# Weight halves split inside attention steps, and earlier places for the last two row groups, in a fused embed, text, attention and expert kernel

## What is computed

```
h = concat(patch_embedding(x), text_layers(x_txt))            # 32 x 114 x 256
h = h + attention(layernorm(h))                               # causal, 128-wide q and k
n = layernorm(h)
logits = n @ w_router.T;  top_vals, top_idx = top_k(logits, 2)
rw = softmax(top_vals)
y_e = (silu(n @ w_gate[e].T) * (n @ w_up[e].T)) @ w_down[e].T    # e = 0..7, FFN 512
out = sum over the two chosen e of rw * y_e
h = h + (layernorm(out) * ln_gamma + ln_beta)
```

## Time and profile before

| | us |
|---|---|
| median of 3 runs | 1122.44 (1122.32 to 1122.86) |
| the profiled execution: its time | 1125.7 |
| the profiled execution: span from first to last instruction | 1123.9 |
| busy in that span: PE, DVE, ACT, POOL | 975.9, 758.9, 601.9, 577.5 |
| mean granted TensorE clock, as a share of full speed | 0.939 |

### The profile page before, as it was taken

The page is one execution under the profiler, slowest core; times in us unless marked ns, Lnnn a source line. Parts: engine busy times, 40 slices in busy tenths (PEclk is TensorE's granted clock), DMA queues, the critical chain, the costliest instruction groups (busy, mean ns, idle before and its releaser), DMA issues.

```text
span 1123.9 us, 20592 instructions
## 1 busy us (share of the span) xinstructions
PE 975.9 (87%) x5838; PEld 846.4 (75%) x5839; DVE 758.9 (68%) x1966; ACT 601.9 (54%) x1343; POOL 577.5 (51%) x630
## 2 busy tenths in 40 slices
PE   5878999999999999999898962499999999999910
PEld 4668999999999999998666652377777777777710
DVE  1666999999999998998678767244444444444447
ACT  1466776877788777666697753123223223223223
POOL 4523765567667766777627767232222222222236
PEclk8998999999999999999999975699999999999965
DMA  9451001000100000012168236133233333333263
GB/s 278 130 151 57 1 1 66 1 2 1 67 1 2 1 25 2 10 58 57 36 212 260 61 76 224 52 47 50 47 47 49 49 47 47 47 50 48 43 162 118
DMA packets 54733, 75.49 MB, mean 67 GB/s; under 512 B 9348, under 2 KB 46978, under 8 KB 52612
## 3 DMA queue, kind: packets, MB, share of 16 engines
q1 hardware_dynamic: 32680, 49.24, 14.5%
q0 software_dynamic: 16640, 18.53, 10.1%
q10 hardware_dynamic: 5340, 6.83, 2.2%
HBM read 45.38 MB, written 29.14 MB: 66 GB/s over the span
## 4 chain that ended last, share of the span: by engine, by line
PE 68%; DVE 10%; POOL 7%; DMA 5%; issue 4%; ACT 3%; SPq 2%; POOLq 0%; ACTq 0%; DVEq 0%
PE bank L1264 16%; PE bank L1580 10%; PE bank L1329 7%; PE bank L1557 6%; PE bank L1566 5%; PE bank L1565 4%; PE bank L1324 3%; POOL xrows L1174 3%; PE bank L1560 3%; PE bank L1572 2%; DMA xtok<-in_tok_emb,tokens_s 2%; PE bank L1312 2%; SPq L541 1%; POOL xtok L1052 1%; DVE arena_b L1736 1%
## 5 line engine op out<-in xcount | busy, mean ns | idle before, releaser
L1203 POOL DMA_INDIRECT yrows<-arena_b,dest_i x64 | 99.2, 1550 | 268.2 <-ACT arena_b L1009 260.3
L1736 DVE SCALAR_TENSOR_TENSOR arena_b<-bank,sml,arena_b 128x304 f32<-128x304 f32 (+2 forms) x384 | 195.3, 522 | 20.7 <-ACT arena_b L778 17.9
L1264 PE MATMUL bank<-xt_hi,w_hi 128*128 128x308 f32 x512 | 159.9, 312 | 4.6 <-DVE arena_b L1736 3.2
L1264 PE MATMUL bank<-xt_hi,w_lo 128*128 128x308 f32 x512 | 157.3, 307 | 0.0
L1264 PE MATMUL bank<-xt_lo,w_hi 128*128 128x308 f32 x512 | 156.9, 306 | 0.0
L2057 DVE TENSOR_TENSOR arena_b<-bank,arena_b 128x512 f32<-128x512 f32 x64 | 44.3, 691 | 140.5 <-PE bank L1566 76.7
L1090 POOL TENSOR_TENSOR u_halves<-arena_b,u_halves 128x308 fp32r<-128x308 f32 x128 | 109.8, 865 | 29.8 <-ACT arena_b L790 29.7
L1084 POOL TENSOR_TENSOR y_lo<-arena_b,y_hi 128x308 fp32r<-128x308 f32 x128 | 107.9, 857 | 27.2 <-ACT y_hi L802 27.0
L1264 PEld LDWEIGHTS bank<-xt_hi,w_hi 128*128 128x128 f32 x512 | 98.0, 191 | 5.4 <-DVE arena_b L1736 3.5
L1580 PE MATMUL bank<-arena_b 128*128 x384 | 98.7, 393 | 1.2 <-DVE arena_b L2073 0.9
L1264 PEld LDWEIGHTS bank<-xt_hi,w_lo 128*128 128x128 f32 x512 | 98.0, 191 | 0.0
(11 more groups left out here) (212 smaller groups left out, 2650.3 us busy)
## 6 DMA issues: line engine op xcount, KB each, us to landing
arena_b<-xrows SPq DMA_DIRECT2D x64, 129.5 KB, 2.1
wg_raw<-in_w_gate SPq DMA_DIRECT2D x4, 1024.0 KB, 7.1
yrows<-arena_b SPq DMA_DIRECT2D x1, 3648.0 KB, 18.7
h_all<-seq SPq DMA_DIRECT2D x8, 448.0 KB
w_raw<-in_w_in SPq DMA_DIRECT2D x3, 1024.0 KB, 4.8
arena_b<-in_w_down SPq DMA_DIRECT2D x3, 1024.0 KB, 8.6
wu_raw<-in_w_up SPq DMA_DIRECT2D x2, 1024.0 KB, 7.3
wu_s<-in_w_up SPq DMA_DIRECT2D x2, 1024.0 KB, 9.4
```

The costliest lines, as they stand in the source:

```text
L1203: pool.indirect_dma_start(yrows, bass.IndirectOffsetOnAxis(ap=dest_i[:, m:m + 1], axis=0), f_y[m % 2], None, compute_op=ALU.add).then_inc( ...
L1264: mm = pe.matmul(out_, in_half(w, layer, d, slice(c * P, (c + 1) * P)), x[:, d, cols], start=(k == 0), stop=(k == len(pairs) - 1))
L1736: dve.scalar_tensor_tensor(acc[:, :, back_:TXT], x[:, :, 0:TXT - back_], conv_w(s // GROUPS, c, tap), acc[:, :, back_:TXT], ALU.mult, ALU. ...
```

## The change

It does three things.

1. Pieces 0 to 3 of the weights are split inside the attention steps: ACT does 0 and 1 in step 2 and 2 and 3 in step 3, behind the first norm of the next group and ahead of the tanh. DVE does piece 0 in step 2 ahead of the choice, piece 1 at the end of step 2, pieces 2 and 3 in steps 3 and 4 ahead of the choice.
2. Pieces 4 and 5 stay behind the table on DVE, but wait now until POOL has issued its last row send (the semaphore `pad_zero` gets a new name and a second increment for that). PE waits for four pieces before its first block and for the other two before the up product of block 0.
3. From step 8 on, the ranks and the places of a group stand in the same step as its choice, behind it: group 6 in step 8 and group 7 in step 9, where they stood one step later. Step 8 keeps the places of group 5 at its start.

```diff
--- before.py
+++ after.py
@@ -336,7 +336,9 @@
         assert at[0] <= 3 * FC * GT
 
         EMBEDDED = 5
-        SPLIT_FIRST = 3
+        SPLIT_FIRST = 4
+        SPLIT_STEP = 2
+        LOWER_AT = {2: 0, 3: 2, 4: 3}
         BIAS_OPS = 3 * 3 + 11
         LAST_LAG = 3
         SENT_FIRST = 5
@@ -472,7 +474,7 @@
         a_om, a_h2 = sem("a_om"), sem("a_h2")
         m_stats, m_rstd, m_norm, m_tr, m_trc = sem("m_stats"), sem("m_rstd"), sem("m_norm"), sem("m_tr"), sem("m_trc")
         m_lm, m_gap, m_wt, m_both, m_rk = sem("m_lm"), sem("m_gap"), sem("m_wt"), sem("m_both"), sem("m_rk")
-        m_slot, pad_zero = sem("m_slot"), sem("pad_zero")
+        m_slot, zeroed_then_sent = sem("m_slot"), sem("zeroed_then_sent")
         a_bias, m_bias, ld_qkv = sem("a_bias"), sem("m_bias"), sem("ld_qkv")
         x_sent = [sem(f"x_sent{k}") for k in range(ROW_SETS)]
 
@@ -966,6 +968,9 @@
                     key(g)
                 if has(g + 1):
                     norm_rows(g + 1)
+                if g in (SPLIT_STEP, SPLIT_STEP + 1):
+                    for k in range(2):
+                        upper_weights((g - SPLIT_STEP) * 2 + k)
                 if has(g - 2):
                     weight(g - 2)
                 if has(g):
@@ -976,9 +981,6 @@
                     rows_turned(g + 1, 1)
                 if has(g):
                     gate_values(g, 1)
-                if g - 1 == GROUPS - 1:
-                    for k in range(SPLIT_FIRST):
-                        upper_weights(k)
                 if has(g - 1):
                     routed_norm(g - 1)
 
@@ -1185,7 +1187,7 @@
                 if has(g + 2):
                     norm_ahead(g + 2)
                 if g == 0:
-                    pool.memset(padbuf[:, :], 0.0).then_inc(pad_zero, 1)
+                    pool.memset(padbuf[:, :], 0.0).then_inc(zeroed_then_sent, 1)
                 if has(g - 1):
                     routed_scale(g - 1)
                 if has(g - 3):
@@ -1194,6 +1196,8 @@
             for g in range(GROUPS + LAST_LAG):
                 attn_step(g)
 
+
+            settled(pool, zeroed_then_sent)
 
             def send(j, m, landed):
                 pool.wait_ge(f_yc, j + 1)
@@ -1507,7 +1511,7 @@
                 if has(g - 2):
                     turn_routed(g - 2, 0)
                     turn_routed(g - 2, 1)
-                if has(g - 3):
+                if has(g - 3) and g <= GROUPS:
                     ranks(g - 3)
                 if has(g):
                     values(g, 0)
@@ -1525,6 +1529,8 @@
                     values(g, 1)
                 if has(g + 1):
                     bias_scores(g + 1)
+                if has(g - 2) and g >= GROUPS:
+                    ranks(g - 2)
 
             bias_scores(0)
             for g in range(GROUPS + LAST_LAG):
@@ -1537,7 +1543,7 @@
 
             pe.wait_ge(tbl_ready, 2)
             pe.wait_ge(ld_ffn, 16 * (len(FFN_PIECES) + FC))
-            pe.wait_ge(w_lower, len(FFN_HALVES))
+            pe.wait_ge(w_lower, SPLIT_FIRST)
 
             def turn_block(j, k, turn_):
                 pe.wait_ge(x_in[k], turn_ * 16 + 16)
@@ -1561,6 +1567,8 @@
                 mm.then_inc(f_gm, 1)
                 wait(pe, f_hh, j)
                 pe.wait_ge(f_raw, j + 1)
+                if isinstance(j, int) and j == 0:
+                    pe.wait_ge(w_lower, len(FFN_HALVES))
                 for x, w in ((x_lo, wu_hi), (x_hi, wu_hi), (x_hi, wu_lo)):
                     pe.matmul(bank[1][:, :], x[:, k, 0, :], w[:, cols], start=(x is x_lo), stop=False)
                 pe.matmul(bank[1][:, :], x_raw[k], wu_s[:, cols], start=False, stop=True).then_inc(f_um, 1)
@@ -1915,7 +1923,7 @@
 
             def routed_stats(g):
                 if g == 0:
-                    dve.wait_ge(pad_zero, 1)
+                    dve.wait_ge(zeroed_then_sent, 1)
                     dve.tensor_copy(padbuf[:, D:D + 1], cst[:, C_PADDEST:C_PADDEST + 1]).then_inc(pad_ready, 1)
                     for half in range(2):
                         dve.wait_ge(seq_stored[2 + half], 16 * len(rows_out[half]) * GROUPS // 2)
@@ -1982,15 +1990,14 @@
 
             text_iterations(text_step)
             def attn_step(g):
-                if has(g - 3):
+                if has(g - 3) and g <= GROUPS:
                     place_rows(g - 3)
                 if has(g + 1) and g:
                     norm_bias(g + 1)
                 if has(g + 2):
                     norm_ahead_stats(g + 2)
-                if g - 2 == GROUPS - 1:
-                    for k in range(SPLIT_FIRST):
-                        lower_weights(k)
+                if g in LOWER_AT:
+                    lower_weights(LOWER_AT[g])
                 if has(g - 2):
                     choose(g - 2)
                 if has(g):
@@ -2003,9 +2010,13 @@
                     count(g - 2)
                 if has(g - 1):
                     routed_bias(g - 1)
+                if has(g - 2) and g >= GROUPS:
+                    place_rows(g - 2)
                 if has(g):
                     invert(g)
                     weigh(g)
+                if g == SPLIT_STEP:
+                    lower_weights(1)
 
             for g in range(GROUPS + LAST_LAG):
                 attn_step(g)
@@ -2046,6 +2057,7 @@
             dve.tensor_copy(expert_i[:, :], expert_f).then_inc(tbl_ready, 1)
             c.done()
             dve.wait_ge(tbl_ready, 2)
+            dve.wait_ge(zeroed_then_sent, 2)
             for k in range(SPLIT_FIRST, len(FFN_HALVES)):
                 lower_weights(k)
```

## The result

The changed kernel takes **1137.07 us** (median of four, 1131.94 to 1140.74), the kernel before beside it 1122.43: a ratio of **1.0116** (95% interval 1.0095 to 1.0138), slower by 14.6 us. Two further sets of the same kernel, taken later on two chips, gave 1.0135 and 1.0131. The forecast was 1133.5, with a range of 1130.0 to 1138.5: the time is inside, and 3.6 us above the point.

A forecast was written before the change was run, and what follows sets the result against it. The bound was taken as a ring of ACT, PE and DVE, then POOL's row sends from 682 us. A shift of +18.2 less 7.1 at the end gave +11.1 us: median 1133.5, range 1130 to 1138.5.

The forecast's parts named there:

- The stall: Step 2: ACT stands 8.0 us for the first two weight loads; with the copies the ring shifts 12.0 us.
- The other pieces: Piece 1's lower half and pieces 2 and 3, steps 2 to 4: shift grows from 12.0 to 18.2 us.
- The shift at the end of step 4: Total delay of the attention steps from the stall and pieces 0 to 3: 18.2 us.
- The end: POOL's last sends, up to the first expert transpose: 2.1 us of idle and slowed sends go, 7.1 us gained.
- all six are now alone: End: the six sends formerly beside pieces 0 to 5 meet no lower half, saving 2.7 and 2.3 us.
- The slow sends: POOL sends beside DVE's lower halves: pieces 2 and 3 lengthen one or two sends, 0.8 to 1.6 us a piece.
- The sum: Whole kernel: +18.2 us of shift less 7.1 us at the end, +11.1 us, median 1133.5.
- The clock: PE's granted clock after its idle time in step 2: counted as nothing, ACT and DVE hiding a slow PE.
- The rival: Clock stays low in two or three steps where PE is waited for: +3 to +5 us, 1136.5 to 1138.5; chance 0.11.
- The other rivals: No stall (1125.5, chance 0.05); no gain at the end (1140.6, 0.05); not slower, by packed sends (1122.8, 0.07).
- the ring: Attention steps, first half: ACT, PE and DVE release each other, 14.5 us a step, no engine alone the bound.
- packing its queue: Not-slower rival: POOL's sends packed without waits for slots give back 10.7 us, about 1122.8; chance 0.07.

The follow-up runs named there:

- the profile with the memset: Changed kernel, with the bare increment that frees DVE's pieces 4 and 5 replaced by a small POOL memset behind its last send: 1135.96 us, ratio 1.0110.
- the repeated run: The changed kernel again without an edit, on two chips: 1140.87 us, ratio 1.0135, and 1138.83 us, ratio 1.0131.

## Why the prediction was right, and where it was not

**The stall: right.** 8.0 us were worked out from when SP issues its third load; 8.00 were measured, released by the load named. The exact hit is luck: the wait was 7.83 and 8.24 us in the changed kernel's other profiles, and 6.09 and 6.78 in two others with the same pieces in step 2. Step 2 is 12.6 us longer (the tanh comes 12.2 later, 12.0 were forecast; the rest is part of piece 1). With the pieces one step later the stage is 6.8 us shorter than in the profile after, though its clock fell for longer in step 4.

**The other pieces: right, a little too large.** Steps 3 and 4 together are 5.0 us longer; 6 was forecast. The shift at the end of step 4 is 17.6 us (18.2). The first send comes at 597.72, which with the 5.1 us of the text stage added is 602.8 (603).

**The end: one step failed.** "Pieces 4 and 5 wait for the end of POOL's last send" and "all six are now alone" are not what the semaphore does. The increment was done at least eleven microseconds ahead of the last send's end, and the pieces slowed two sends by 2.1 us. The Trainium skill (PSUM — Partial Sum Buffer, section "Engine vs sequencer instructions") gives the reason: a bare semaphore operation runs on the sequencer and doesn't wait for the instructions ahead of it to complete. The trace agrees (DVE at 704.98, last send to 716.15), and a write in its place gave the forecast order. With that write the end gains 7.4 us, where 7.1 was forecast; as changed it gains 5.2 in two profiles and 6.2 in the first. There the clock fell 15.3 us after the start of step 7, in the other two 13.0 and 13.3; this may be the 1 us, which wasn't tried.

**The slow sends: the price was right, the reading behind it wrong.** The prediction asked whether a lower half holds a send up wholly, and said that the rows, 0.8 to 0.9 us a send, do not bear it out. They do. In all 14 profiles each of the 59 sends that start while a lower half runs ends 1.0 us after the end of that half: the one at 663.02 above ends at 665.28, its half at 664.28. Such a send is held until the half is over. It loses what is left of the half when it starts, 0.8 to 1.6 us, and not the whole 2.28, since mostly an earlier send was under way when the half began. A send that is under way is not lengthened (1.11 to 1.15 us), nor is the half (2.26 to 2.32). The page that the prediction named (the Trainium skill, SBUF — State Buffer, "SBUF: two separate sides") has whichever side comes second blocked wholly. The trace agrees for a send that starts during a half, and does not for a half that starts during a send. The sum took no harm, as its prices were measured ones.

**The sum, by the profiled execution: right.** +11.3 us against +11.1, the 0.6 us less shift and the 0.9 us less gain of the end almost cancelling out. So close a hit is partly luck, and it holds for this execution, whose clock fell briefly, and not for the other two that were profiled.

**The clock: the term that was mis-sized.** "I count nothing, since ACT and DVE are late in step 3 and hide a slow PE" nearly holds for step 3 (18.39 us where its dip was gone, 18.85 to 19.26 with it), and the short dip of step 5 was there before as well. It fails for the long fall in step 5: there TensorE is waited for, and in two of three profiles the step takes 21.0 us, 4.9 more than before. With 1.0 at the end, and in one of them 0.6 more in step 2, that makes +17.3 and +17.9. Judged by the mean clock, some nine of fifteen executions are of this kind, which would put the median between, as it is: 14.6 us over before, or 15 to 17 in the later sets. The rival was priced at 3 to 5 us, about right, but at a chance of 0.11, far too little; that the median still lies inside the range is owed to the upper end, which this rival had set. Whether the pause ahead of step 5 (2.33 us, ahead of the turns) brings the fall is open: the profile with the memset has the pause (2.31 us) and no fall in that step. Why a fall lasts four times as long in some executions is not shown. The profile of the kernel before has no long one, and none of its 49 executions on three chips a mean clock under 0.937.

**The other rivals** fell by their own conditions: the loads had not landed, the end did gain, and POOL's slots came as late as the ring, so packing its queue gave nothing back beyond that.

## What to carry to other kernels

Work that needs a load goes behind the point where that load lands by the trace, not where the engine has a gap: a wait in an in-order queue holds everything behind it. Where a producer is a chain of its own (here POOL's sends), its idle time and its slowed instructions are the gain to look for, and the helpers that slow it go ahead of its last stretch or truly behind it, signalled by an instruction of its datapath. A delay in one step also opens pauses in TensorE, and what a low clock may cost after them belongs into the sum, for the step in which TensorE is waited for. One profile can show the short case by chance; here it took three to see the long one.

## What was not expected of the hardware

Behind a pause of about the same length (2.29 to 2.33 us, ahead of step 5's turns) the granted clock fell for 3.4 us in one profile of the changed kernel, for 13.7 in two, and with the memset not at all in that step. TensorE was recorded as busy throughout the short fall (3.42 of 3.42 us) and the long one (13.66 of 13.66). The Trainium skill (TensorE: Matmul & The Clock Gate, "What's actually happening") has activity lift the clock; these records don't tell the short fall from the long.

A send that starts during a lower half is held until that half ends, and one that is under way is not: where the first send starts decides what a half costs.

The opening of the program spreads too. The mean clock of the first 128 us was 0.95 in the first profile after, 0.92 before and 0.91 in the repeated run, and the attention stage began at 541.37, 546.45 and 545.99. In all 14 profiles the two go together: the stage began at 540.1 to 542.2 us where that clock was 0.95, at 542.3 to 543.7 at 0.93, and at 545.5 to 546.5 at 0.92 or 0.91. It may be what separates executions of the kernel before (1119.6 to 1127.5 us over three chips); that wasn't tried. It is why stages, not end times, were compared.
